# GpSimd instead of SyncE issues the transfers of the expert weights, with new orders of stages

## The chip, the cores and the metric

The kernel runs on one core of one Trainium2 chip. A core has five engines with an instruction stream each: TensorE (PE), VectorE (DVE), ScalarE (ACT), GpSimd (POOL) and SyncE (SP). SP computes nothing here; it issues DMAs. ACT and POOL can issue DMAs too. Each engine takes its stream in order: an instruction that waits for a semaphore holds up all that stand behind it on the same engine. The metric is device time in microseconds for one execution; lower is better.

## The reference

The program is two layers over eight sequences of 256 tokens with 128 features, all in float32. Cut to what matters:

```
xn = layernorm(x)
x  = x + attention_block(xn) + cell(xn)      # layer 0
xn = layernorm(x)
x  = x + mamba_block(xn) + moe(xn)           # layer 1

attention_block: 2 x (B=2, L=128 reshaped), 16 heads of 8, softmax(q k^T) + position table, Wo,
                 normalise, W1, W2, normalise
cell:            6 nodes in a chain; each: 8-head attention (q, k, v from earlier nodes),
                 output projection, weighted skip; layernorm at the end
mamba_block:     u = ln(x); in_proj; conv of 4 taps; silu; dt, B, C; scan over 16 states of
                 256 channels; gate; out_proj; + u; h = ln; gelu(h W1 + b1) W2 + b2; + residual
moe:             router over E = 8 experts, softmax(logits / 1.5), top 2 weights per token;
                 every expert is computed: h = silu(xn W1[e]); y = h W2[e];  out = sum_e w_e y
```

W1[e] and W2[e] are 128 x 512 and 512 x 128 floats, 256 KB each. Every expert is applied to every sequence, so 8 x 8 pairs of such matrices are brought in over the run.

## The kernel before

The eight sequences run as a pipeline. For each sequence b the work is cut into stages that stand in lanes (`CELL`, `SIDE`, `RAW`, `LAYER1`, `EXPERTS`, and `FOLD` once at the start). `ON` says which engines take part in a stage of a given name. For each engine the table `ORDER` holds one letter per stage: A to H are the cell's stages of sequences 0 to 7, a to h the key and value projections, I to P the attention block, i to p the mamba block and the FFN, Q to X the experts, and - the one-time folding. The function `order` takes the next stage of the letter's lane that this engine has a part in. So the order of work on each engine is fixed by hand or by a planner ahead of time, and the semaphores only make it correct. `BANKS` gives each use of a small PSUM bank its number (three banks `ps`), in TensorE's order.

The expert weights go through a ring of three buffers (`RING = 3`, tiles `w_e1` and `w_e2`, both called `w_e` in the trace). The stage `weights(b, e)` is number i = 8 b + e. It waits until the second product of expert i - 3 has been computed, since that frees the buffer, and then starts two transfers of 256 KB. TensorE's stage `expert(b, 2e)` waits for both of them:

```
def weights(b, e):
    i = b * EX + e
    if i == 0: sp.wait_ge(*fold_done.at(0, 2 * NODES - 1))
    if i >= RING: ready(sp, (i - RING) // EX, ("y", (i - RING) % EX))
    sp.dma_start(w_e1[:, i % RING, :], t["w_e1"][:, e, :]).then_inc(weights_in[i % RING], 16)
    sp.dma_start(w_e2[:, i % RING, :, :], ...).then_inc(weights_in[i % RING], 16)
```

In the trace these are SP's lines L623 and L624. Expert e's products are TensorE's lines L980 (first, stage `expert`) and L968 (second, stage `expert_y`, which frees the buffer).

What else SP issues: `load` and `store` of a sequence, the spreading of the attention block's heads through DRAM (`t_rows`, `a_write`, `a_stack`, `v_read`, `o_write`, `o_read`), and `rows` (L602), 128 times. `rows` closes a chain that every group of four heads goes through twelve or four times per sequence: TensorE computes scores into the four-bank PSUM tile `strips` (stage `max`, L772), VectorE takes their maximum (stage `top`, L1322, `rowmax`), TensorE transposes it (L779), ScalarE copies it out (L1080, `maxrow`), SP's `rows` moves its 4 KB into spare partitions of `qs_b` or `qs_a`, and TensorE computes the scores again with the maximum subtracted (stage `score`, L787). ScalarE then takes the exponential (stage `exp`, L1087, `probs`), which frees `strips`, and TensorE multiplies by the values (L800).

What GpSimd does: small operations that stand between two of VectorE. `root` (L1596) turns a variance into 1/sqrt for each of seven normalisations: `n0`, `n1` and `n2` are those of the second layer, and VectorE's `apply` (L1301) waits for it; `n1`'s result goes to TensorE's `z_t` (L882), `n2`'s to `h_t` (L936). `n0_apply` (L1625) and `x2` (L1661, L1663) sum residuals, `conv` (L1635) does the first tap, `dtx` (L1641) a product, and `state` (L1648, L1654, L1656) adds the halves of each pair of states; VectorE's `state(b, k)` (L1449) waits for the sum of pair k - 2.

## Time and profile before

| | |
|---|---|
| time, median of 3 executions | 1353.74 us (1352.81 to 1356.07) |
| the profiled execution | 1361.48 us |
| its span, first to last instruction | 1359.7 us |
| mean granted TensorE clock | 0.939 of full speed |
| PE busy | 1145.5 us, 84% |
| DVE busy | 988.0 us, 73% |
| ACT busy | 747.5 us, 55% |
| POOL busy | 272.9 us, 20% |
| expert weights | 128 transfers of 256 KB |

The profile is of one execution, so sums are made against its 1361.48 us; the median of the unprofiled ones is 7.7 us lower. Busy time counts neither waiting nor the issuing of DMAs. In a timeline row the number in brackets is the idle time of the engine ahead of the instruction, with what ended it.

### The profile page before, as it was taken

The page shows a single profiled execution, that of the slowest core. Times are in us where ns is not written, and L with a number is a line of the kernel's source. Part 1 is how long each engine was busy: PE and PEld are TensorE (multiplying, and loading weights), DVE is VectorE, ACT ScalarE, POOL GpSimd, SP SyncE. Part 2 cuts the span into 40 slices and gives each one's busy share as a digit, 9 for nine tenths or more (in the row PEclk, how much of TensorE's full clock was granted, in tenths as well). Part 3 has the DMA queues.
Part 4 walks back from the last instruction along what each step waited for, and adds up shares of the span by engine and source line. Part 5 has one row for each costly group of instructions (what it writes and reads, how often), then busy time and mean ns, then how long its engine had stood idle before and what let it go on. Part 6 is the DMA issues. An engine that isn't in the chain of part 4 may idle for free.

```text
span 1359.7 us, 27149 instructions
## 1 busy us (share of the span) xinstructions
PE 1145.5 (84%) x10384; PEld 781.7 (57%) x10384; DVE 988.0 (73%) x1563; ACT 747.5 (55%) x1325; POOL 272.9 (20%) x262
## 2 busy tenths in 40 slices
PE   6587768878988799988997899889998899888677
PEld 4354444545765567655764566656665567656455
DVE  3143245797678977897777877899677978788796
ACT  2233444664657565866567565665557565654442
POOL 1000002152022322043022232124112411023200
PEclk9787797889999899999999899899999899979799
DMA  7620011000310112110320031100310121002010
GB/s 210 145 60 1 2 39 23 2 17 29 95 40 17 28 68 57 35 33 17 75 68 2 17 81 42 52 32 28 92 37 2 48 76 52 33 32 71 4 62 20
DMA packets 117517, 62.66 MB, mean 46 GB/s; under 512 B 79440, under 2 KB 99440, under 8 KB 117392
## 3 DMA queue, kind: packets, MB, share of 16 engines
q1 hardware_dynamic: 113488, 54.68, 14.8%
q10 hardware_dynamic: 3904, 6.26, 1.4%
q8 instruction: 85, 1.39, 0.4%
q14 instruction: 40, 0.33, 0.1%
HBM read 53.56 MB, written 6.83 MB: 44 GB/s over the span
## 4 chain that ended last, share of the span: by engine, by line
PE 57%; DVE 20%; issue 10%; ACT 9%; DMA 3%; POOL 1%; SPq 0%; ACTq 0%; DVEq 0%; POOLq 0%
PE strips L787 9%; PE strips L772 8%; PE attn_out L800 7%; PE ps L968 6%; DVE rowmax_B L1322 6%; PE ps L980 6%; ACT probs L1087 4%; DVE hb L1457 3%; DVE rowmax_A L1322 2%; PE ps L823 2%; DVE hb L1449 2%; DVE hb L1464 2%; PE ps L911 2%; PE ps L730 2%; PE ps L890 1%
## 5 line engine op out<-in xcount | busy, mean ns | idle before, releaser
L1087 ACT ACTIVATE probs<-strips 128x2048 f32<-128x2048 f32 x128 | 240.2, 1877 | 108.8 <-PE strips L787 108.3
L1322 DVE TENSOR_REDUCE rowmax_B<-strips 128x8 f32<-128x2048 f32 x96 | 219.5, 2286 | 90.7 <-PE strips L772 89.8
L1457 DVE TENSOR_TENSOR_SCAN hb<-da,hb 128x1024 f32<-128x1024 f32 x64 | 156.9, 2452 | 2.5 <-ACT da L1171 0.8
L980 PE MATMUL ps<-ze,w_e 128*128 128x256 f32 x512 | 140.1, 403 | 8.8 <-DVE hb L1464 2.5
L787 PE MATMUL strips<-qs_b,ks_b 32*128 32x256 f32 x1536 | 120.4, 430 | 23.1 <-ACT probs L1087 13.0
L772 PE MATMUL strips<-ks_b,qs_b 32*128 32x256 f32 x1536 | 117.0, 420 | 26.0 <-ACT probs L1087 12.7
L968 PE MATMUL ps<-w_e,work 128*128 128x128 f32 x1024 | 133.0, 286 | 3.5 <-DVE hb L1449 1.1
L968 PEld LDWEIGHTS ps<-w_e,work 128*128 128x128 f32 x1024 | 126.6, 200 | 13.7 <-issue 10.5
L1171 ACT ACTIVATE da<-dt,a_neg 128x255 f32<-128x255 f32 x256 | 108.0, 498 | 24.3 <-DVE hb L1457 23.9
L1654 POOL TENSOR_TENSOR cv_t<-hb 128x512 f32<-128x512 f32 x49 | 62.4, 1273 | 275.5 <-DVE hb L1464 275.5
L1218 ACT ACTIVATE eh_t<-ps 128x512 f32<-128x512 f32 x128 | 74.8, 594 | 74.7 <-PE ps L980 74.0
L980 PEld LDWEIGHTS ps<-ze,w_e 128*128 128x128 f32 x512 | 93.2, 197 | 38.5 <-issue 19.9
L1561 DVE SCALAR_TENSOR_TENSOR work<-eh_t,ps 128x512 f32<-128x512 f32 x128 | 85.3, 678 | 36.0 <-ACT eh_t L1218 35.7
L800 PE MATMUL attn_out<-probs,vb 128*32 128x256 f32 x1536 | 108.3, 404 | 0.6 <-ACT probs L1087 0.2
L772 PEld LDWEIGHTS strips<-ks_b,qs_b 32*128 32x128 f32 x1536 | 75.0, 194 | 52.9 <-issue 48.1
L787 PEld LDWEIGHTS strips<-qs_b,ks_b 32*128 32x128 f32 x1536 | 76.6, 199 | 48.1 <-issue 30.9
L1656 POOL TENSOR_TENSOR cv<-cv,cv_t 128x512 f32<-128x512 f32 x49 | 92.0, 1878 | 3.8
L1080 ACT ACTIVATE maxrow<-ps 8x128 f32<-8x128 f32 x128 | 33.7, 264 | 105.8 <-PE ps L779 104.0
L1322 DVE TENSOR_REDUCE rowmax_A<-strips 128x8 f32<-128x2048 f32 x32 | 73.1, 2286 | 24.6 <-PE strips L772 24.5
L1464 DVE TENSOR_TENSOR hb<-hb,ps 128x1024 f32<-128x1024 f32 x64 | 77.7, 1214 | 13.6 <-PE ps L911 12.9
L1449 DVE TENSOR_TENSOR hb<-ps,dtx 128x1024 f32<-128x1024 f32 x64 | 78.0, 1218 | 12.3 <-PE ps L911 11.2
L800 PEld LDWEIGHTS attn_out<-probs,vb 128*32 128x32 f32 x1536 | 41.7, 113 | 47.6 <-issue 24.1
(239 smaller groups left out, 1825.7 us busy)
## 6 DMA issues: line engine op xcount, KB each, us to landing
w_e<-in_w_e SPq DMA_DIRECT2D x128, 256.0 KB, 2.9
qs_a<-a_scr SPq DMA_DIRECT2D x8, 512.0 KB, 3.8
ks_a<-a_scr SPq DMA_DIRECT2D x8, 512.0 KB, 4.9
pos<-t_scr ACTq DMA_DIRECT2D x16, 192.0 KB
a_scr<-qkv_a SPq DMA_DIRECT2D x16, 128.0 KB, 4.3
qs_b<-maxrow SPq DMA_DIRECT2D x96, 4.0 KB
x_in<-in_x SPq DMA_DIRECT2D x8, 128.0 KB, 2.4
a_scr<-ks_a SPq DMA_DIRECT2D x2, 512.0 KB, 6.5
```

The costliest lines, as they stand in the source:

```text
L772: mm = pe.matmul(o, strip(qs, b, kind, g, j, qc * P, P), strip(ks, b, kind, g, j, 0, L), start=True, stop=True)
L787: mm = pe.matmul(o, strip(ks, b, kind, g, j, kc * P, P), strip(qs, b, kind, g, j, 0, L), start=True, stop=True)
L800: mm = pe.matmul(attn_out[32 * j:32 * j + 32, i * L:(i + 1) * L], v, heads[:, j, kc, :], start=(kc == 0), stop=(kc == 1))
L968: mm = pe.matmul(o[:, h * D:(h + 1) * D], eh[:, e % 2, j, h * P:(h + 1) * P], w_e2[:, (b * EX + e) % RING, j, :], start=(j == 0), stop=(j ...
L980: mm = pe.matmul(o[:, j * L:(j + 1) * L], w_e1[:, n % RING, f * P:(f + 1) * P], ze[:, b % 2, :], start=True, stop=True)
L1087: act.activation(probs[:, group % 2, :, :, :].rearrange("p h a b -> p (h a b)"), strips[:, :], ACT.Exp).then_inc(s_exp, 1)
L1171: last = act.activation(da[:, k % 2, m, j, 1:L], dt[:, m, 1:L], ACT.Exp, scale=a_neg[:, m, 2 * k + j:2 * k + j + 1])
L1322: dve.tensor_reduce(out=rowmax[kind][:, b % sides_n, k % 2, :, :], in_=strips[:, :].rearrange("p (h q t) -> p h q t", h=4, q=2), axis=AX, ...
L1449: dve.tensor_tensor(hk, o, dtx[:, :, :].unsqueeze(2).to_broadcast([P, CH, 2, L]), ALU.mult).then_inc(hb_done.of(b), 1)
L1457: dve.tensor_tensor_scan(flat_h, flat_a, flat_h, 0.0, ALU.mult, ALU.add).then_inc(scan_done.of(b), 1)
L1464: dve.tensor_tensor(hk, hk, o, ALU.mult).then_inc(hc_done.of(b), 1)
L1656: pool.tensor_tensor(ysum[:, :, :], ysum[:, :, :], pair[:, :, :], ALU.add).then_inc(ysum_done.of(b), 1)
```

## The change

`weights` moves from SP to GpSimd. The function is the same but for the engine: it waits for the same semaphores and starts the same two transfers with the same counts. No computation is added or removed. With it come new tables `ORDER` for all five engines and new `BANKS`.

```diff
 ON = {
-    "sync": "load rows t_rows a_write a_stack v_read o_write o_read weights store",
+    "sync": "load rows t_rows a_write a_stack v_read o_write o_read store",
...
-    "gpsimd": "consts prep_root xn_bo end_root ... conv dtx state x2",
+    "gpsimd": "consts prep_root xn_bo end_root ... conv dtx state x2 weights",
...
 ORDER = {
     "sync": (
-        "IAAAIIIIIIJJJJJABBQAQQIIBAAI...
+        "IAAIAIIIIIJJJJJAABBIAIAIBAAAAI...
...
     "gpsimd": (
-        "ABIJCK-IIIIAAiiiDLiiiiiiiiiiiiJJBJBJjjjEM...
+        "ABIJCQQQ-IIKIIAAiiiDLiiiiiiiQiiQiiiQQQJJRBJBJRjjjEM...
...
-                sp.dma_start(w_e1[:, i % RING, :], t["w_e1"][:, e, :]).then_inc(weights_in[i % RING], 16)
-                sp.dma_start(w_e2[:, i % RING, :, :], t["w_e2"][:, FF * e:FF * e + FF, :]).then_inc(weights_in[i % RING], 16)
...
+                    pool.wait_ge(*fold_done.at(0, 2 * NODES - 1))
+                if i >= RING:
+                    ready(pool, (i - RING) // EX, ("y", (i - RING) % EX))
+                pool.dma_start(w_e1[:, i % RING, :], t["w_e1"][:, e, :]).then_inc(weights_in[i % RING], 16)
+                pool.dma_start(w_e2[:, i % RING, :, :], t["w_e2"][:, FF * e:FF * e + FF, :]).then_inc(weights_in[i % RING], 16)
```

Leaving the 64 `weights` stages out, the number of stages that stand at another place in their engine's sequence is 97 of 216 on SP, 455 of 1362 on TensorE (126 of them by two places or more, the farthest by 16), 303 of 921 on ScalarE, 170 of 842 on VectorE (by at most 6) and 19 of 185 on GpSimd. Three places of these sequences follow. Lines behind the removed function have other numbers in the changed kernel: GpSimd's L1596 is L1587 there, L1625 is L1616, L1635 is L1626, L1661 and L1663 are L1652 and L1654; its L1662 and L1663 are the two transfers.

SP, near the start: in the kernel before, the first three `weights` stages stand among the `rows` of sequences 0 and 1.

```order
35 L575 DMA a_scr<-qkv_a 128x16x16 x2
36 L576 DMA v_scr<-qkv_a 128x256
37 L602 DMA qs_b<-maxrow 4x2x128 x2
38 L623 DMA w_e<-in_w_e 128x512
39 L624 DMA w_e<-in_w_e 128x512
40 L602 DMA qs_b<-maxrow 4x2x128
41 L623 DMA w_e<-in_w_e 128x512
42 L624 DMA w_e<-in_w_e 128x512
43 L623 DMA w_e<-in_w_e 128x512
44 L624 DMA w_e<-in_w_e 128x512
45 L602 DMA qs_a<-maxrow 4x2x128 x2
```

In the changed kernel, at the same place:

```order
37 L575 DMA a_scr<-qkv_a 128x16x16 x2
38 L576 DMA v_scr<-qkv_a 128x256
39 L602 DMA qs_b<-maxrow 4x2x128 x3
40 L602 DMA qs_a<-maxrow 4x2x128
41 L602 DMA qs_b<-maxrow 4x2x128
42 L602 DMA qs_a<-maxrow 4x2x128
```

Nothing stands between these index transfers any more.

GpSimd, the first two normalisations of layer 1 of sequence 6 (`n0_root`, `n0_apply`, `n1_root`, then `conv`). Before:

```order
217 L1596 TENSOR_TENSOR rstd_n<-veps_n,half_neg 128x2
218 L1625 TENSOR_TENSOR res<-x,u 128x256
219 L1596 TENSOR_TENSOR rstd_n<-veps_n,half_neg 128x2
220 L1635 TENSOR_SCALAR cv<-xi,convw 128x256 x2
221 L1641 TENSOR_TENSOR dtx<-dt,xc 128x512
```

Changed:

```order
313 L1587 TENSOR_TENSOR rstd_n<-veps_n,half_neg 128x2
314 L1616 TENSOR_TENSOR res<-x,u 128x256
315 L1662 DMA w_e<-in_w_e 128x512
316 L1663 DMA w_e<-in_w_e 128x512
317 L1662 DMA w_e<-in_w_e 128x512
318 L1663 DMA w_e<-in_w_e 128x512
319 L1587 TENSOR_TENSOR rstd_n<-veps_n,half_neg 128x2
320 L1662 DMA w_e<-in_w_e 128x512
321 L1663 DMA w_e<-in_w_e 128x512
322 L1626 TENSOR_SCALAR cv<-xi,convw 128x256 x2
```

The stages `weights(6, 0)` and `weights(6, 1)` now stand between the sum of the residual and the root of `n1`, and `weights(6, 2)` behind it.

GpSimd, the end of layer 1's mamba block of sequence 4 (`x2`, then `n2_root`). Before:

```order
177 L1661 TENSOR_TENSOR res<-res,u 128x256
178 L1663 TENSOR_TENSOR res<-res,rows 128x256
179 L1596 TENSOR_TENSOR rstd_n<-veps_n,half_neg 128x2
180 L1596 TENSOR_TENSOR rstd_wo<-veps_wo,half_neg 128x2
181 L1610 TENSOR_TENSOR ab_bias<-rem_a,bias_ff 128x256
```

Changed:

```order
251 L1652 TENSOR_TENSOR res<-res,u 128x256
252 L1654 TENSOR_TENSOR res<-res,rows 128x256
253 L1662 DMA w_e<-in_w_e 128x512
254 L1663 DMA w_e<-in_w_e 128x512
255 L1587 TENSOR_TENSOR rstd_n<-veps_n,half_neg 128x2
256 L1662 DMA w_e<-in_w_e 128x512
257 L1663 DMA w_e<-in_w_e 128x512
```

`weights(4, 5)` now stands ahead of the root of `n2`, and `weights(4, 6)` behind it.

## Rows read from the trace of the kernel before

**Rows 1.** The page: busy time of engines, and shares of the ending chain.

```profile
PE 1145.5 (84%) x10384; PEld 781.7 (57%) x10384; DVE 988.0 (73%) x1563; ACT 747.5 (55%) x1325; POOL 272.9 (20%) x262
PE 57%; DVE 20%; issue 10%; ACT 9%; DMA 3%; POOL 1%; SPq 0%; ACTq 0%; DVEq 0%; POOLq 0%
```

**Rows 2.** The page, DMA issues: count, KB each, us to landing (median).

```profile
w_e<-in_w_e SPq DMA_DIRECT2D x128, 256.0 KB, 2.9
```

**Rows 3.** Timeline of SP from 85.9 us: start, duration, engine, line, operation.

```profile
85.90 0.36 SPq L623 DMA_DIRECT2D w_e<-in_w_e  x1
86.30 0.43 SPq L624 DMA_DIRECT2D w_e<-in_w_e  x1
86.77 0.53 SPq L602 DMA_DIRECT2D qs_b<-maxrow  x1
```

**Rows 4.** Timeline of ACT at the same place, then of PE.

```profile
83.09 0.27 ACT L1080 ACTIVATE maxrow<-ps 8x128 f32<-8x128 f32 x1 [1.10 <-PE ps L779]
85.32 1.88 ACT L1087 ACTIVATE probs<-strips 128x2048 f32<-128x2048 f32 x1 [0.72 <-PE strips L787]
...
89.18 2.09 PE L787 MATMUL strips<-qs_b,ks_b 32*128 32x256 f32 x16 [1.78 <-DMA qs_b<-maxrow]
```

**Rows 5.** Timelines near 632 us (ACT, SP, PE) and near 785 us (ACT, PE).

```profile
631.75 0.27 ACT L1080 ACTIVATE maxrow<-ps 8x128 f32<-8x128 f32 x1 [1.91 <-PE ps L779]
...
632.49 0.53 SPq L602 DMA_DIRECT2D qs_b<-maxrow  x1
...
635.27 0.93 PE L787 MATMUL strips<-qs_b,ks_b 32*128 32x256 f32 x12 [1.21 <-DMA qs_b<-maxrow]
...
783.83 1.88 ACT L1087 ACTIVATE probs<-strips 128x2048 f32<-128x2048 f32 x1 [0.85 <-PE strips L787]
...
785.85 0.93 PE L787 MATMUL strips<-qs_b,ks_b 32*128 32x256 f32 x12 [1.87 <-ACT probs L1087]
```

**Rows 6.** The waits: who for whom, us in total, times, longest.

```profile
PEld strips L787 <- DMA qs_b<-maxrow: 11.4, 11, 2.0
```

**Rows 7.** POOL by line (busy us, mean ns), then one tile (ns min/median/max).

```profile
L1596 POOL TENSOR_TENSOR rstd_n<-veps_n,half_neg 128x2 f32<-128x2 f32 x24 | 16.9, 704 | 21.9 <-DVE veps_n L1296 21.1
...
L1656 POOL TENSOR_TENSOR cv<-cv,cv_t x49: 1259/1271/3148, 280.0 to 1254.7; 128x512 f32<-128x512 f32 x49
```

**Rows 8.** Timelines of POOL, PE and DVE, 1134 to 1143 us (sequence 6).

```profile
1134.88 0.73 POOL L1625 TENSOR_TENSOR res<-x,u 128x256 f32<-128x256 f32 x1 [0.82 <-DVE u L1301]
1136.46 0.70 POOL L1596 TENSOR_TENSOR rstd_n<-veps_n,half_neg 128x2 f32<-128x2 f32 x1 [0.86 <-DVE veps_n L1296]
...
1135.47 1.95 PE L968 MATMUL ps<-w_e,work 128*128 128x128 f32 x16
...
1142.38 0.38 PE L882 MATMUL ps<-ident,z_tm 128*128 128x128 f32 x2
...
1138.51 0.59 DVE L1301 TENSOR_SCALAR z_tm<-u,mv_n,rstd_n 128x128 f32<-128x128 f32 x2
```

**Rows 9.** Timelines of POOL and PE, 948 to 951 us (sequence 4).

```profile
948.25 0.72 POOL L1663 TENSOR_TENSOR res<-res,rows 128x256 f32<-128x256 f32 x1
949.08 0.70 POOL L1596 TENSOR_TENSOR rstd_n<-veps_n,half_neg 128x2 f32<-128x2 f32 x1
...
950.75 0.44 PE L936 MATMUL ps<-ident,z_tm 128*128 128x128 f32 x2
```

**Rows 10.** Timelines of POOL and PE, 846 to 852 us (expert 7, sequence 3).

```profile
846.64 0.69 POOL L1596 TENSOR_TENSOR rstd_prep<-veps_prep,half_neg 128x2 f32<-128x2 f32 x1 [1.78 <-DVE veps_prep L1296]
...
850.89 1.46 PE L980 MATMUL ps<-ze,w_e 128*128 128x256 f32 x6
```

**Rows 11.** Timelines of PE and DVE, 459 to 472 us (sequence 1).

```profile
459.93 3.75 PE L968 MATMUL ps<-w_e,work 128*128 128x128 f32 x16 [0.45 <-ACT maxrow L1080]
...
471.49 1.23 DVE L1449 TENSOR_TENSOR hb<-ps,dtx 128x1024 f32<-128x1024 f32 x1
```

85 lines of the change are left out of this document (41 added, 44 removed).

## The prediction, made before the changed kernel was run

> **What bounds the kernel.** I read the page first: PE is busy 84% of the span, DVE 73%, POOL 20%, and of the chain that ended last PE holds 57%, DVE 20%, DMA 3%, POOL 1% and SP's own issuing nothing that shows [rows 1]. So no single engine is saturated, but TensorE is close, and whatever makes it idle, or makes VectorE idle ahead of a stage that feeds it, is time. Both engines run in a fixed order, so a stage that comes late holds up all behind it, whether or not other work is ready. POOL's 20% says only that it has room; it doesn't say that it has room at the right moments, and that is the question here. Next I read the transfers: 128 of 256 KB, landing 2.9 us after their issue [rows 2]. In the waits nobody waits for one of them, so bringing the weights in is hidden today. The change can therefore help only through what stood behind the weights on SP, and can hurt only through what stands behind them on POOL, through weights that arrive later, and through the new orders.
>
> **SP is freed.** The change takes 64 stages off SP, with two issues of 0.36 and 0.43 us each [rows 3], and the wait ahead of them. Of the 128 index transfers `rows`, 34 stand directly behind such a pair. The clearest case is at the start. ScalarE had the row ready at 83.09 + 0.27 = 83.36 us, but SP stood in `weights(0, 0)` until 85.9 and issued it at 86.77. TensorE began the scores at 89.18 after 1.78 us of idleness, which this transfer ended [rows 3, 4]. Now the index goes out at 83.4 and is there 2.41 us later (89.18 - 86.77), at 85.8. What is late next is `strips`: the exponential holds it until 85.32 + 1.88 = 87.20 [rows 4], and TensorE's earlier work ended at 89.18 - 1.78 = 87.40. So the whole gap goes: -1.8 us. A second case is near 632 us: row ready at 632.02, issued at 632.49, a gap of 1.21 us in TensorE [rows 5]. The lag is the smaller, so this gives -0.5. The third that looks like one is not: near 785 us the gap of 1.87 us was ended by the exponential, which ran until 785.71 [rows 5]; an earlier index changes nothing there. The other `rows` behind a pair were issued in time or have their `score` well behind. Sum on SP: -2.3 us.
>
> **The price of an issue on POOL.** No DMA is issued from POOL in this trace. From below: SP's issue, 0.43 us [rows 3]. It cannot be less, or the weights would be issued for nothing. From above: the longest operation that POOL shows, 3.13 to 3.15 us, where the same addition otherwise takes 1.27 [rows 7]. I take 1.1 us: the smallest arithmetic on POOL, on 2 elements per partition, takes 0.70 [rows 7], which is what an instruction costs there before it does anything, and 0.4 for the issue itself. A stage of two issues is then 2.2 us, and 64 of them are 141 us, so POOL goes from 20% to some 30%. Most of that lies in time when POOL waits anyway. The last word of a pair lands 2.9 - 0.43 = 2.5 us behind the second issue [rows 2, 3].
>
> The Trainium skill, "DMA: Bandwidth & Descriptors", section Specifications, gives a first byte after about 1 us for the GpSimd path and about 0.6 us for SyncE's. By that estimate each landing would be 0.4 us later than I count, which would add 0.4 us to the sum below; no row here shows it.
>
> **Where it lies on POOL's path.** For each of the 64 stages I set the moment at which its buffer comes free against the operation that now stands behind it on POOL. In most places nobody notices. An example: `weights(1, 4)` stands ahead of `state(1, 4)` and has to wait for a product that ended at 459.93 + 3.75 = 463.68. POOL's pair sum comes out at 463.68 + 2.2 + 1.27 = 467.2. The one who waits for it is VectorE's `state(1, 6)`, at 471.49 [rows 7, 11]. 4 us are left, so it costs nothing; with 3.13 us an issue it would be 471.2, still just nothing. Three places are different.
>
> First, sequence 6, 1135 us [rows 8]. `weights(6, 0)` begins when the residual sum is done, 1134.88 + 0.73 = 1135.61, and ends at 1137.81. `weights(6, 1)` may begin at 1135.47 + 1.95 = 1137.42, so it follows at once and ends at 1140.01. `n1_root` ends at 1140.71. VectorE used it at 1138.51, so VectorE stands still for 2.2 us, with the experts' gating and the next maximum queued behind, for which TensorE waits in turn. TensorE's `z_t` at 1142.38 has itself moved a few places forward, so it hides nothing. +2.2 us.
>
> Second, sequence 4, 949 us [rows 9]. `weights(4, 5)` begins at 948.25 + 0.72 = 948.97, its buffer being long free, and `n2_root` starts at 951.17 instead of 949.08. VectorE's scaling follows in the same instant, and TensorE's `h_t` came at 950.75, directly on its heels. +2.1 us. That expert 5 itself (just behind `h_t`) gets its weights at 951.17 + 2.5 = 953.7 lies mostly under the same delay.
>
> Third, sequence 3, 847 us [rows 10]. `weights(3, 7)` is issued only behind the root of another sequence, at 846.64 + 0.69 = 847.33, and lands at 847.33 + 2.2 + 2.5 = 852.03. TensorE wants it at 850.89. +1.1 us.
>
> Sum on POOL: +5.4 us. With 0.43 us an issue the three are 0.5, 0.9 and 0: +1.4. With 3.13 us they are 10.3, 6.2 and 5.2: +21.7.
>
> **The new orders.** 455 of TensorE's 1362 stages and 170 of VectorE's 842 have moved, nearly all by a place or two among neighbours that don't depend on each other. At the start the order of TensorE is practically the old one, and the attention block of sequence 0 has the same transfers ahead of it. I find no place where a large gap is closed or opened. I count zero, with bounds on both sides: a neighbour in the wrong place costs, or gives back, a gap such as 1.78, 1.21 or 1.87 us [rows 4, 5], and some five more of one sign than of the other are easily possible, so 8 us each way.
>
> **Sum.** -2.3 + 5.4 + 0 = +3.1 us. The profiled execution took 1361.5 us, which becomes 1364.6; the median of the runs is 7.7 us lower, 1353.7, which becomes 1357 us. With the lowest price it is 1353.7 - 2.3 + 1.4 = 1352.8.
>
> **Rivals.**
>
> POOL's issues are dear (slower). If each takes as long as a blocked POOL operation, 3.13 us, the sum is 1353.7 - 2.3 + 21.7 = 1373 us, and places that I count as hidden come to light too. For it: the 3.15 us in rows 7 are the same operation as the 1.26 us ones, so POOL can be held up by something outside of it. Against it: the median there is 1.27, so most are not. It decides from about 1.3 us an issue on, where the result passes 1358. The Trainium skill, "SBUF — State Buffer", section SBUF: two separate sides, states a rule of this sort against the change: a DMA from the GpSimd queue has its descriptors written by GpSimd, which can't write them while VectorE holds the port that they share, whereas those from SyncE are immune. By that rule alone the result would be this rival's 1373; no run so far shows a DMA under it.
>
> The index transfers gain much more (faster). TensorE's loading of weights for L787 waited 11.4 us in 11 places for them [rows 6]. If a queue free of 256 KB transfers in front lets all of that go, and if half of the 8 us of the orders comes on top, it is 1353.7 - 11.4 - 4 + 3 = 1341 us. Against it: I found only two of these waits behind a pair; the others are the transfer's own time.
>
> SP was never in the way (no change). The transfers run on the same DMA engines whoever starts them, and if both POOL's delays and SP's lags are taken up by the slack between stages, the time stays at 1354. The Trainium skill, "DMA: Bandwidth & Descriptors", section Issuing engines are not separate DMA queues, says just this: another issuing engine saves only the time to initiate.
>
> The orders decide (either sign): 1353.7 ± 8, 1346 or 1362.
>
> **Chances.** A measurement of this kernel can tell about 0.3%, 4.1 us, from no change. My forecast (1352.8 to 1360) gets 0.40: 0.24 within 0.3%, 0.14 slower, 0.02 faster. Dear issues 0.20, all slower. Index transfers 0.16, all faster. No change 0.09. The orders 0.15: 0.06 faster, 0.02 within, 0.07 slower. Together: faster 0.24, same 0.35, slower 0.41. The range has to take in the upper price and most of the faster cases: 1343 to 1374.
>
> **What would show it.** Right: SP shows no wait of L623's kind and `score(0, 3)` starts near 87.4 us instead of 89.2; POOL's transfers take about 1.1 us each, POOL's busy time with them is near 410 us; `n1_root` of sequence 6 and `n2_root` of sequence 4 stand directly behind an issue and VectorE has a gap of some 2 us ending on them; TensorE waits a few us in all for `w_e`, where it waited for none. Wrong: issues of 2 us or more, or of very unequal length beside VectorE's scans (the dear rival); waits of L787 for the index gone altogether (the faster one); or gaps of TensorE that moved to lines which have to do with neither SP nor POOL, in which case the orders decided and my zero for them was the mistake.

## The result

The changed kernel took 1361.00 us (median of 5 runs, 1360.25 to 1363.86) against 1353.74 (1352.81 to 1356.14, 5 runs) before. The ratio is 1.0047, with a 95% interval of 1.0029 to 1.0066: slower by about 6.4 us by the ratio (the two medians lie 7.3 us apart), which is more than 0.3%, and 4 us above the predicted 1357.

The two profiled executions, 1360.8 us after and 1361.5 before, don't show this. The one before lies 7.7 us above its median, at a mean granted clock of 0.939, the one after at 0.953. A single execution of this kernel scatters: 35 runs of the kernel before on one chip spread from 1349.2 to 1364.1 us (standard deviation 3.5 us). So what follows compares medians for the sum, and traces only for stretches that repeat from one execution to the next.

The page of the changed kernel: busy time by engine, then the chain that ended last [answers to rows 1], then the transfers of the weights by issue and by queue [rows 2].

```profile
PE 1131.6 (83%) x10384; PEld 768.2 (57%) x10384; DVE 985.9 (73%) x1563; ACT 747.5 (55%) x1325; POOL 346.3 (25%) x390
...
PE 51%; DVE 20%; issue 11%; ACT 10%; DMA 5%; POOL 2%; SPq 0%; ACTq 0%; DVEq 0%; POOLq 0%
...
w_e<-in_w_e POOLq DMA_DIRECT2D x128, 256.0 KB, 3.1
```

PE's busy time fell by 13.9 us (1145.5 to 1131.6), as less of it ran at the half clock, and the time did not: the span less the busy time, PE's idleness, rose from 214.2 to 227.4 us. POOL has 128 instructions and 73.4 us more, 0.57 us for each. The queue's share of the chain is small throughout.

The transfers by line, with durations in ns (minimum, median, maximum); L1662 is the first and L1663 the second issue of a stage. Below L1663: who waited for it, and how long its landing took:

```profile
L1662 POOL DMA_DIRECT2D w_e<-in_w_e x64: 536/579/701, 85.8 to 1335.3; - x64
...
L1663 POOL DMA_DIRECT2D w_e<-in_w_e x64: 536/536/555, 86.5 to 1335.9; - x64
...
  PEld ps L971: 0.6, 1
  PE ps L971: 0.4, 1
...
DMA to landing us min/median/max: 3.0/3.3/6.2
```

An issue takes 0.54 to 0.58 us, half of the 1.1 that I had counted, and never more than 0.70. This speaks against the dear rival. The Trainium skill, "SBUF — State Buffer", section SBUF: two separate sides, has GpSimd kept from writing descriptors while VectorE runs an operation in a two-port mode. None of the 128 issues here shows it, and no landing took more than 6.2 us, where SyncE's took up to 5.1 us in the kernel before and up to 7.6 with the new orders. Whether an issue ever met such an operation was not looked up, so this doesn't test the rule.

The first place of SP (timelines of ACT, SP, PE and POOL, start and duration in us), to be held against rows 3 and 4:

```profile
82.66 0.27 ACT L1071 ACTIVATE maxrow<-ps 8x128 f32<-8x128 f32 x1 [1.10 <-PE ps L770]
82.95 1.14 SPq L602 DMA_DIRECT2D qs_b<-maxrow  x2
...
86.91 1.15 PE L778 MATMUL strips<-qs_b,ks_b 32*128 32x256 f32 x16
...
85.76 0.70 POOL L1662 DMA_DIRECT2D w_e<-in_w_e  x1 [41.06 <-DVE bias_v L1242]
86.46 0.54 POOL L1663 DMA_DIRECT2D w_e<-in_w_e  x1
```

SP now issues the index 0.02 us behind the row instead of 3.4, and `score(0, 3)` starts at 86.91 instead of 89.18. In the waits, TensorE's loading of weights waited 4.7 us in 8 places for such an index, against 11.4 in 11 [rows 6]. Most of this fall isn't SyncE's freedom. The new orders with the weights on SyncE (below) have 4.2 us in 6 places, and start `score(0, 3)` without a wait too, since SyncE's own new order has the weights behind the index; the move alone has 7.1 in 10. And the same wait for the other tile, `qs_a`, grew:

```profile
PEld strips L787 <- DMA qs_a<-maxrow: 3.8, 4, 1.5
```

```profile
PEld strips L778 <- DMA qs_a<-maxrow: 6.5, 5, 1.7
```

So of 15.2 us for both tiles 11.2 are left.

### The profile page after: what moved, and what is told of

The parts are those of the page before. It is cut to its first block, busy times and chain, and to the rows that moved or that the text cites. A ratio compares the mean times of both kernels' runs of the same rounds, so it can differ in the third digit from the quotient of the medians.

```text
span 1359.0 us, 27149 instructions
## 1 busy us (share of the span) xinstructions
PE 1131.6 (83%) x10384; PEld 768.2 (57%) x10384; DVE 985.9 (73%) x1563; ACT 747.5 (55%) x1325; POOL 346.3 (25%) x390
## 3 DMA queue, kind: packets, MB, share of 16 engines
q0 software_dynamic: 10240, 33.56, 7.2%
## 4 chain that ended last, share of the span: by engine, by line
PE 51%; DVE 20%; issue 11%; ACT 10%; DMA 5%; POOL 2%; SPq 0%; ACTq 0%; DVEq 0%; POOLq 0%
PE strips L778 8%; PE strips L763 8%; PE attn_out L791 6%; DVE rowmax_B L1313 5%; PE ps L959 5%; ACT probs L1078 4%; PE ps L971 4%; DVE rowmax_A L1313 2%; PE ps L814 2%; DVE hb L1448 2%; DVE hb L1440 1%; PE ps L902 1%; ACT da L1162 1%; PE attn_out L798 1%; DVE hb L1455 1%
## 5 line engine op out<-in xcount | busy, mean ns | idle before, releaser
L1448 DVE TENSOR_TENSOR_SCAN hb<-da,hb 128x1024 f32<-128x1024 f32 x64 | 152.8, 2388 | 2.4 <-ACT da L1162 0.8
L959 PE MATMUL ps<-w_e,work 128*128 128x128 f32 x1024 | 128.3, 279 | 2.9 <-ACT ze L1128 0.8
L959 PEld LDWEIGHTS ps<-w_e,work 128*128 128x128 f32 x1024 | 122.1, 193 | 12.8 <-issue 10.5
L1647 POOL TENSOR_TENSOR cv<-cv,cv_t 128x512 f32<-128x512 f32 x49 | 94.3, 1925 | 3.8
L1440 DVE TENSOR_TENSOR hb<-ps,dtx 128x1024 f32<-128x1024 f32 x64 | 78.1, 1220 | 16.5 <-PE ps L902 13.9
L1662 POOL DMA_DIRECT2D w_e<-in_w_e x64 | 36.7, 573 | 157.4 <-PE ps L959 47.1
```

Of the source, the lines that this page charges most:

```text
L959: mm = pe.matmul(o[:, h * D:(h + 1) * D], eh[:, e % 2, j, h * P:(h + 1) * P], w_e2[:, (b * EX + e) % RING, j, :], start=(j == 0), stop=(j ...
L1440: dve.tensor_tensor(hk, o, dtx[:, :, :].unsqueeze(2).to_broadcast([P, CH, 2, L]), ALU.mult).then_inc(hb_done.of(b), 1)
L1448: dve.tensor_tensor_scan(flat_h, flat_a, flat_h, 0.0, ALU.mult, ALU.add).then_inc(scan_done.of(b), 1)
L1647: pool.tensor_tensor(ysum[:, :, :], ysum[:, :, :], pair[:, :, :], ALU.add).then_inc(ysum_done.of(b), 1)
```

## Undoing it part by part

The orders can be cut. At many points the same stages lie ahead of the point in both orders, on all five engines at once, so that a kernel can run the one order up to there and the other behind it. I used a point at 846 us of the changed kernel's trace (VectorE about to start `inproj` of sequence 4). The tables below are one row of `ORDER` each; the other engines' rows and `BANKS` go with them.

**The kernel before once more**, for the scatter of traces.

> The kernel before, unchanged, profiled a second time. The first profiled execution took 1361.5 us, 7.7 us over the median of its kernel, with a mean granted clock of 0.939; the changed kernel's took 1360.8 with 0.953. If the first was merely an execution with a low clock, this one comes out near 1354 us with a clock of 0.945 or more, and the 7 us between the two kernels are to be read against it. If profiled executions of this kernel are always longer, it comes out near 1361 again, and the comparison of the two traces on record (equal spans) is a fair one.

It took 1356.72 us, span 1354.9, 4.8 us shorter than the first trace of the same kernel, at a mean granted clock of 0.938: neither of the two outcomes expected. The difference comes in steps of either sign, of 0.6 to 3.1 us from the end of one `ffn_out` to the next.

**The move alone**: GpSimd issues, old orders and old banks.

```diff
 ORDER = {
 ...
-        "TPUmmUmmmUmUUmmmmmUmUNNNUNFFnnnVVnVnnnnVVnnnVnnnnVVOOGOOGooWWoWooWooWWoooWPWPooXXPoXPHHoopppppXXXXXpppppppppp",
+        "TPUmmUmmmUmUUmmmmmUmUNNNUNFFnnnVVnVnnnnVVnnnVnnnnVVOOGOGOooWWoWooWooWWoooWPWPooXXPoXPHHoopppppXXXXXpppppppppp",
 ...
```

> The move alone: the weights are issued by GpSimd, with the orders of before on TensorE, ScalarE, VectorE and SyncE (less the 64 weights stages) and its PSUM banks; on GpSimd the stages stand in the order of before, with the weights behind the same neighbours as in the changed kernel. Theory A (the new orders cost the time, the move is free: an issue took 0.54 to 0.58 us and nobody waited for weights but 1 us): 1351 to 1356 us, a ratio of 0.998 to 1.002 to before. Rival B (the move costs it, through what waits on GpSimd behind a weights stage): 1359 to 1363 us. If each has a part, between them.

**The new orders alone**: SyncE issues, new orders and banks.

```diff
 ORDER = {
 ...
-        "nnnOOGOGOooooooooooPPooPoPHHooppppppppppppppp",
+        "nnnOOGOOGooooooooooPPooPoPHHooppppppppppppppp",
 ...
```

> The orders alone: the new orders of the changed kernel on TensorE, ScalarE, VectorE and GpSimd and its PSUM banks, but the weights issued by SyncE, standing among its other stages by the moments at which GpSimd issued them in the trace of the changed kernel. Theory A (the new orders cost the time): 1359 to 1363 us. Rival B (the move costs it): 1352 to 1356 us.

The move alone gave 1359.59 us, ratio 1.0027 (1.0005 to 1.0048). The new orders alone gave 1362.65, ratio 1.0054 (1.0033 to 1.0076). Both together are the changed kernel, 1.0047. So the orders alone already make the whole loss, theory A of that run, and with them in place the move adds nothing that can be seen. But the move in the old orders is not free, as theory A of its run had it: its interval lies above 1, and its time is that of rival B. The two parts don't simply add (0.27 and 0.54% against 0.47 together), though the difference, 0.34%, is about as large as its uncertainty. In the orders-alone kernel the weights stand at new places on SyncE, too, so it holds the whole of the new order and not the old places of the weights. Stage by stage against the trace of the kernel before, both kernels with new orders were ahead at 850 us and behind at 1125, hence the next pair.

**New orders up to 846 us, old behind it** (GpSimd issues; a row of SyncE's order against the changed kernel):

```diff
-        "MNMNEEOOOOONFHFNTGFFGNFFNGFFNONOGOUGGOPPPPPHHGGGGOOGGHOOPPHPHVHPPHHPHHPPHHWX",
+        "MNMNEEOOOOONFHFTNGFFGFNFNGFOFNNGOPPPPPOGUGHHOGGGGOOPGGHOOHPPVHHPPHHPHHPPHHWX",
```

> The new orders and banks up to 846 us (the place where VectorE goes on to sequence 4's inproj), the old ones from there; weights issued by GpSimd throughout. The traces of the changed kernel and of the new orders with SyncE both lie ahead of the kernel before at 850 us (12.6 and 6.3 us) and behind it at 1125 us (1.5 and 6.2). Theory A (the new orders gain early and lose in 850 to 1125): the early gain stays and the late loss goes, about 1351, between 1347 and 1355. Rival B (the differences of the traces are the spread of single executions and the clock, not the orders): as the changed kernel, 1359 to 1362. Rival C (the loss is what the early gain turns into, because something later waits on a rate that no order moves): 1357 to 1361 as well, but with the milestone at 850 us ahead and the one at 1125 us not.

**Old up to 846 us, new behind it**:

```diff
-        "MNMNEEOOOOONFHFNTGFFGNFFNGFFNONOGOUGGOPPPPPHHGGGGOOGGHOOPPHPHVHPPHHPHHPPHHWX",
+        "MMNENOOOOOENFFHNTGFFGNFFNGFFNONOGOUGGOPPPPPHHGGGGOOGGHOOPPHPHVHPPHHPHHPPHHWX",
```

> The mirror image: old orders and banks up to 846 us, new ones from there; weights issued by GpSimd throughout. Theory A: no early gain, and the whole late loss of 8 to 12 us: 1364 to 1369. Rival B: 1359 to 1362. Rival C (a rate that no order moves): 1357 to 1361.

They gave 1356.70 us, ratio 0.9989 (0.9969 to 1.0010), and 1365.36, ratio 1.0056 (1.0034 to 1.0078). The late half of theory A holds: the same issuing engine, the same set of stages, and 0.67% between the two halves put together in the one way and in the other. B and C, which gave the second kernel at most 1362, fall. The early half of A isn't shown: the first kernel missed its 1347 to 1355, its ratio includes 1, and in its trace sequence 3 ends at 835.6 us, where the kernel before has 836.1 and 835.4.

**New up to 846 us, old behind it, SyncE issues**:

```diff
-        "MEMNNNNNMTTGTFEFSEMEETMFFETEMMMNENTOOOOOENTFFHTUTNUGUFFGUUFNFNUUGFOFUNNGOPPPPPVOGUGVHVHOGGGVGOVVOPGGHOOVVHPPWWWVHHPWWPHHWPWHHPPWHXHXXWXXXXXX",
+        "MMNNNNSNMFTGTTFEESMEEMFFTETEMMNMNEEOOOOOTTNFHFTUTNUGUFFGUUFNFNUUGFOFUNNGOPPPPPVOGUGVHVHOGGGVGOVVOPGGHOOVVHPPWWWVHHPWWPHHWPWHHPPWHXHXXWXXXXXX",
```

> As the run with the new orders up to 846 us and the old ones from there, but with the weights issued by SyncE, at the places of the new-orders-with-SyncE kernel in the early part and of the kernel before in the late one. Theory A with a move that costs 0.2 to 0.3% in the late old order: 1350 to 1353, below the kernel before (1355 to 1357 in its runs here). Rival (the early orders gain only together with the move, since SyncE is then free): as before, 1354 to 1358.

1355.24 us, ratio 0.9994 (0.9970 to 1.0018). The expected 1350 to 1353 did not come, the rival's 1354 to 1358 did. It is no faster than the kernel before, and no version in this study is.

With seven kernels, the one before included, each part of the change can be priced three times, as the difference of two ratios that differ in it alone:

| part | pairs | mean |
|---|---|---|
| new orders behind 846 us | +0.29, +0.58, +0.60% | +0.49%, +6.6 us |
| new orders up to 846 us | -0.38, -0.09, -0.06% | -0.18%, -2.4 us |
| GpSimd issues | +0.27, -0.05, -0.07% | +0.05%, +0.7 us |

One difference is uncertain by some 0.3%, a mean of three by not quite 0.2%. So the late part is shown, and the early part and the move are each not told from nothing (the one price of the move that stands clear of nothing by itself is that in the old orders, +0.27%). The traces say the same of the late part. Us by stretch, from one end of `ffn_out` to the next (each row a single execution):

| kernel | to 3 | 3 to 4 | 4 to 5 | 5 to 7 |
|---|---|---|---|---|
| before, its two traces | 836.1, 835.4 | 129.6, 128.6 | 159.9, 160.5 | 230.8, 227.1 |
| move alone | 832.3 | 131.2 | 162.4 | 233.8 |
| new then old, GpSimd | 835.6 | 130.5 | 160.9 | 227.4 |
| new then old, SyncE | 830.7 | 129.4 | 161.2 | 228.4 |
| old then new, GpSimd | 830.2 | 132.6 | 166.0 | 226.2 |
| new orders, SyncE | 833.8 | 131.5 | 166.5 | 226.8 |
| changed kernel | 827.5 | 131.1 | 168.5 | 228.7 |

From `ffn_out` of sequence 4 to that of 5, the last three rows, which run it in the new orders, are 3.6 to 8.6 us above all others. That is the stretch to read. From 3 to 4 they are longer too against those with the same issuing engine, by 1.0 us on average with GpSimd and 2.3 with SyncE, and from 5 to 7 there is nothing to see within the scatter.

## What happens in the stretch: sequence 5, `bc`

Set against the end of `ffn_out(4)`, the traces of one order agree stage by stage to 0.1 us for long stretches there. Us by part of the stretch on TensorE (each row a single execution; idle is TensorE's):

| kernel | `ffn_out(4)` to `bcdt(5)` | of it idle | to `state(5, 0)` | to `ffn_out(5)` |
|---|---|---|---|---|
| before, its two traces | 53.4, 53.4 | 3.9, 3.9 | 12.0, 12.0 | 94.5, 95.1 |
| move alone | 53.4 | 3.9 | 14.8 | 94.3 |
| new then old, GpSimd | 53.4 | 3.9 | 12.0 | 95.5 |
| new then old, SyncE | 53.4 | 3.9 | 14.8 | 93.1 |
| old then new, GpSimd | 55.0 | 5.2 | 16.3 | 94.8 |
| new orders, SyncE | 55.2 | 5.7 | 16.0 | 95.3 |
| changed kernel | 56.3 | 5.2 | 16.8 | 95.4 |

The two orders part most in the middle, where the old order itself has 12.0 or 14.8 us depending on the clock, and by 1.6 to 2.9 us before it, in several small waits. The middle holds the one place that the next four runs test. TensorE, timelines of the move alone (old order) and of the changed kernel. L770 is the transpose of a row of maxima, L890 the first product of `bcdt(5)`:

```profile
1016.72 0.27 PE L770 MATMUL ps<-ident,rowmax_A 128*8 128x128 f32 x1
1016.83 0.27 PE L770 MATMUL ps<-ident,rowmax_B 128*8 128x128 f32 x1
1016.93 1.03 PE L890 MATMUL ps<-xc,w_bc 128*96 128x256 f32 x4
```

```profile
1014.77 0.27 PE L770 MATMUL ps<-ident,rowmax_A 128*8 128x128 f32 x1
1014.88 1.03 PE L890 MATMUL ps<-xc,w_bc 128*96 128x256 f32 x4
```

The new order has put `rows(7, B, 1)` behind `max(6, B, 7)`, so `bcdt(5)` starts 0.1 us earlier relative to VectorE's maximum ahead of it. A harmless step forward. But `bcdt` releases two things: VectorE's `bc`, which stands behind that maximum and starts no earlier, and ScalarE's `dt`, which releases POOL's `dtx`, and that is 0.1 us earlier. VectorE and POOL in the kernel before, then in the changed one:

```profile
1022.77 0.42 DVE L1430 TENSOR_TENSOR bc<-cv,cv_t 32x256 bf16<-32x256 f32 x1
...
1022.83 1.48 POOL L1641 TENSOR_TENSOR dtx<-dt,xc 128x512 f32<-128x512 f32 x1 [17.04 <-ACT dt L1160]
...
1025.65 1.15 PE L787 MATMUL strips<-qs_a,ks_a 32*128 32x256 f32 x16 [2.59 <-DVE rowmax_B L1322]
```

```profile
1018.64 1.50 DVE L1421 TENSOR_TENSOR bc<-cv,cv_t 32x256 bf16<-32x256 f32 x1
...
1018.59 1.26 POOL L1632 TENSOR_TENSOR dtx<-dt,xc 128x512 f32<-128x512 f32 x1 [16.45 <-ACT dt L1151]
...
1022.60 1.15 PE L778 MATMUL strips<-qs_a,ks_a 32*128 32x256 f32 x16 [3.58 <-DVE rowmax_B L1313]
```

Before, VectorE's last operation of `bc` began 0.06 us ahead of POOL's product and took 0.42 us (POOL's took 1.48). After, POOL began 0.05 us ahead, and the same operation on 32x256 elements took 1.50 us. The maximum of sequence 6 stands behind it, TensorE waits for that, and its idleness rises from 2.59 to 3.58 us. The Trainium skill, "SBUF — State Buffer", section Who interferes with whom, says that a VectorE instruction with two inputs in SBUF contends with a GpSimd one that reads SBUF, and that issue order decides which of the two blocks; the trace agrees, with 0.42 and 1.50 us for the two orders. (GpSimd's product took 1.26 us where it began first and 1.48 where VectorE did.) In the four traces with the new order at this place (the changed kernel, new with SyncE, old then new, and the one with four issues, below) the longest of these operations is 1.50 us; in all those with the old order there it is 0.42.

Behind this, the clock. Windows from that start of TensorE to the end of `state(5, 0)`: the stretch and its length, busy us (instructions) of PE, PEld, DVE, ACT and POOL, granted clock, DMA share, GB/s. In order: before, the move alone, the changed kernel.

```profile
1025.65:1031.20 5.55, 5.33 (x58) 3.42 (x58) 0.22 (x1) 4.46 (x9) 0.00 (x0) 1.00 0.01 3
```

```profile
1023.47:1031.73 8.26, 8.26 (x60) 5.16 (x61) 1.28 (x2) 4.93 (x10) 0.00 (x0) 0.62 0.01 2
```

```profile
1022.60:1031.67 9.07, 8.46 (x59) 4.42 (x59) 1.28 (x2) 5.20 (x10) 0.00 (x0) 0.62 0.01 3
```

The same work takes 5.55 us at 1.00 (2.4 GHz) and 8.26 at 0.62 (part of it at 1.2 GHz). Since the move alone fell too, after the very idleness of 2.60 us that left the kernel before at 1.00, the longer idleness isn't what takes the clock down, or not alone. The next runs separate the two.

**`dtx` of sequence 5 waits for the end of `bc`** (changed kernel):

```diff
             def dt_x(b):
                 pool.wait_ge(*dt_done.at(b))
+                if b == 5:
+                    pool.wait_ge(*bc_steps.at(b, 4))
```

> The changed kernel with one wait added: in sequence 5 GpSimd's dtx product starts only after VectorE's last operation of bc (L1421). In the four traces that end in the new orders (the changed kernel, new orders with SyncE, old then new, four issues) this 32x256 operation of sequence 5 took 1.50 us where the traces with the old late order show 0.42, GpSimd's dtx having begun 0.05 us ahead of it; PE then sat idle 3.6 us ahead of score A 1 of sequence 6 instead of 2.6, and the granted clock was 0.5 for some 5 us behind it. Theory D (that operation is held up by GpSimd's beside it, and the longer idle takes the clock down; both together are some 4 us of the late loss): L1421 at 0.42 us in every sequence, the idle at 2.6 us, the clock at 1.00, the stretch from the end of ffn_out of sequence 4 to state 0 of sequence 5 shorter by 4, and the whole 1357, about 4 below the changed kernel's 1361. Rival E (the 1.1 us come back but the clock falls all the same, other work in the new order being what makes PE idle): stretch shorter by 1 to 2, whole 1359 to 1360. Rival F (whatever is gained there is taken back behind it): stretch shorter, whole 1361.

Its line, TensorE's start behind it, and the window from that start:

```profile
L1421 DVE TENSOR_TENSOR bc<-cv,cv_t x8: 416/416/418, 247.6 to 1288.3; 32x256 bf16<-32x256 f32 x8
...
1024.59 1.45 PE L778 MATMUL strips<-qs_a,ks_a 32*128 32x256 f32 x16 [2.50 <-DVE rowmax_B L1313]
...
1024.59:1033.44 8.85, 8.59 (x59) 4.51 (x59) 1.29 (x2) 5.20 (x11) 0.00 (x0) 0.61 0.01 3
```

The hold-up is gone (0.42 us), the idleness is back at 2.50, and from `bcdt(5)` to `state(5, 0)` it takes 15.49 us instead of 16.79. The clock fell all the same, to 0.61. So at this place E is right and D isn't: 1.1 us of idleness come back, and the clock is a matter of its own. Further on the trace tells no more: from `ffn_out(4)` to `ffn_out(5)` it takes 168.8 us, the changed kernel 168.5, since 1.7 us more went by ahead of `bcdt(5)`, where the added wait can't act and more of the time was at the half clock. In the whole, 1363.19 us and a ratio of 1.0038 (1.0018 to 1.0058) don't tell 1.1 us from nothing, nor E from F.

**The delay put into the kernel before**:

```diff
                 dve.wait_ge(*bc_steps.at(b, 3))
+                if b == 5:
+                    dve.wait_ge(*dtx_done.at(b))
```

> The kernel before (old orders, SyncE) with the delay put in by hand: in sequence 5 VectorE's last operation of bc waits for GpSimd's dtx, so that it ends some 1.6 us later (dtx ran to 1.1 us behind the end of bc, and 0.4 for the operation itself). Theory D: PE's idle ahead of score A 1 of sequence 6 grows from 2.6 to about 4.2 us, the clock falls to 0.5 behind it, the stretch from ffn_out of sequence 4 to state 0 of sequence 5 is 4 to 5 us longer, and the whole 1358 to 1360 against 1355. Rival E (the delay costs its own length and the clock stays): stretch 1.6 longer, whole 1356.6. Rival F (taken back behind it): 1355.

```profile
1026.99 1.61 PE L787 MATMUL strips<-qs_a,ks_a 32*128 32x256 f32 x9 [4.02 <-DVE rowmax_B L1322]
...
1026.99:1033.75 6.76, 6.76 (x58) 4.20 (x58) 0.49 (x1) 4.61 (x9) 0.00 (x0) 0.77 0.01 2
```

The idleness is 4.02 us, the clock 0.77 in the window, and from `bcdt(5)` to `state(5, 0)` it takes 14.72 us instead of 12.01: the delay of 1.4 and 1.3 of lost clock. That the delay took the clock down isn't shown, since it fell as well in five of the eight traces of the old order without the delay. At the end of the kernel nothing of it is left in the trace (0.5 us less than the first trace of before); 1359.55 us, ratio 1.0013 (0.9989 to 1.0037), takes in D, E and F and settles none.

**`dtx` waits in all sequences, new then old, SyncE**. In the old late order another such meeting stands in sequence 4, where `dtx` begins inside `bc`, which then takes 2.90 us instead of 1.95. The new order doesn't have that one: its `bc` takes 1.95 us in sequence 4 and 3.03 in sequence 5, the old one's 2.90 and 1.95. So over both sequences the meetings of `bc` and `dtx` cost the two orders nearly the same, 1.1 us against 0.95, and they explain the stretch from 4 to 5 better than the loss of the whole.

```diff
                 pool.wait_ge(*dt_done.at(b))
+                pool.wait_ge(*bc_steps.at(b, 4))
```

> The run before with GpSimd's dtx waiting for the end of VectorE's bc in all sequences. In the old late order bc of sequence 4 takes 2.90 us instead of 1.95 since dtx begins inside it; with the wait it should take 1.95, and dtx start 1.9 us later in sequence 4 and 0.35 later in sequences 5 and 6. Theory D: 1 us gained at sequence 4 and nothing lost, so 0 to 1.5 us below its twin; rival (dtx late holds up state 0): 0 to 2 us above it.

1355.67 us, ratio 0.9993 (0.9972 to 1.0014), against 0.9994 without the wait. Its trace takes 128.4 us from `ffn_out` 3 to 4, its twin's 129.4, with `bc` of sequence 4 at 1.95 us, as theory D has it. The medians don't tell the theories apart.

**The old orders put back from 966 to 1125 us alone** (changed kernel, a row of SyncE's order):

```diff
-        "MNMNEEOOOOONFHFNTGFFGNFFNGFFNONOGOUGGOPPPPPHHGGGGOOGGHOOPPHPHVHPPHHPHHPPHHWX",
+        "MNMNEEOOOOONFHFNTGFFGNFFNGFFNONGOPPPPPOGUGHHOGGGGOOPGGHOOHPPHVHPPHHPHHPPHHWX",
```

> The changed kernel with the old orders and banks put back in one stretch alone, from 966 us (ffn_out of sequence 4) to 1125 us (ffn_out of sequence 5); before and behind it the new ones, weights on GpSimd. In the traces this stretch is 6.1 to 9.1 us longer than in the kernel before in the four kernels that run it in the new orders and -0.1 to 2.6 longer in those that run it in the old ones without a delay put in. Theory A (the late loss lies in this stretch): 1354 to 1357, 4 to 7 below the changed kernel's 1361. Rival (the loss lies elsewhere behind 846 us, or what is gained here is taken back by 1258 us): 1359.5 to 1362, with the stretch itself shorter.

The stretch shrank as expected, from 168.5 to 163.0 us. The whole did so by half: 1359.76 us, ratio 1.0020 (0.9999 to 1.0042). Theory A's 1354 to 1357 did not come; the time is that of the rival, which had the stretch shorter and the whole at 1359.5 to 1362. Against the changed kernel's 1.0047 it is 0.27% less, with an uncertainty of some 0.3%, so that between none and all of the late 0.49% can be in this stretch. The rest, if there is one, is behind 846 us in places that I have not found; the table points at 3 to 4, where this trace, too, takes 133.4 us.

Within the stretch I read the loss of some 6 us in the traces as a sum of pieces, of which only the first was tested by a run: 1.1 us of `bc`; 0.6 us where TensorE's second expert product waits for ScalarE (the new order has put `rows(7, B, 1)` behind an exponential there); two further steps of 0.5 to 0.7 and one of 1.5 near `wo_y` of sequences 5 and 6; and the half clock, which came in all five traces that run `bc(5)` in the new order (the one with the wait included) and in six of the nine with the old one, too few to call it the order's.

The largest of TensorE's waits that differ is `wo_y`'s, for the attention block's heads coming back from DRAM. Over the stretch: the move alone, the new orders with SyncE, the changed kernel (the kernel before has none).

```profile
PE ps L850 <- DMA va_hd<-o_scr: 1.1, 1, 1.1
PE ps L859 <- DMA va_hd<-o_scr: 2.9, 2, 2.1
PE ps L850 <- DMA va_hd<-o_scr: 2.0, 2, 1.6
```

In the old orders this is a cost of the move that neither the prediction nor the expectations had. Sequence 6 in the kernel before, then in the move alone:

```profile
1105.33 0.34 SPq L608 DMA_DIRECT2D o_scr<-out_hd  x1
1107.14 0.36 SPq L614 DMA_DIRECT2D va_hd<-o_scr  x1
1107.56 1.14 SPq L623 DMA_DIRECT2D w_e<-in_w_e  x1
```

```profile
1103.20 0.59 POOL L1662 DMA_DIRECT2D w_e<-in_w_e  x1
1104.54 0.34 SPq L608 DMA_DIRECT2D o_scr<-out_hd  x1
1107.77 0.37 SPq L614 DMA_DIRECT2D va_hd<-o_scr  x1
1112.05 0.71 PE L850 MATMUL ps<-waq,va_hd 128*128 128x128 f32 x4 [1.09 <-DMA va_hd<-o_scr]
```

On SyncE the weights stand behind `o_write` (L608) and `o_read` (L614). On GpSimd a pair goes out 1.3 us ahead of `o_write`, which then lands 3.1 us after its issue instead of 1.7; `o_read` waits for that landing and takes 4.2 us itself instead of 3.0. All four kernels with the old order there and GpSimd issuing have this wait (0.9 to 1.1 us), none of the five with SyncE does. No run took it away by itself.

## GpSimd's path: two more runs

**Roots first.** Where an issue stood right ahead of a short POOL stage, that stage goes first (14 stages of weights, 12 places), with the old orders; against the move alone:

```diff
-        "TPUmmUmmmUmUUmmmmmUmUNNNUNFFnnnVVnVnnnnVVnnnVnnnnVVOOGOGOooWWoWooWooWWoooWPWPooXXPoXPHHoopppppXXXXXpppppppppp",
+        "PTUmmUmmmUmUUmmmmmmUUNNNNUFFnnnVVnVnnnnVVnnnVnnnnVVOOGOGOoooWWWooWooWWoooWPPWooXXPoPXHHoopppppXXXXXpppppppppp",
```

> The orders of before with GpSimd issuing the weights, and wherever an issue stood right ahead of a root or another short GpSimd stage that DVE waits for (14 stages of weights in 12 places, n1_root of sequence 6 and n2_root of sequence 4 among them) that stage goes first. Against the move alone with the old orders, 1359.6. Theory P (the move's cost lies in GpSimd stages that run 1.1 to 2.2 us late behind the issues): 1355 to 1357, as before. Rival Q (these places cost nothing, the 4 us are elsewhere or are spread): 1358.5 to 1361.

It took 1362.69 us, ratio 1.0031 (1.0005 to 1.0057), no better than the move alone; P falls. Why shows at sequence 4, which I had named. POOL and PE in the move alone, then PE with the root first:

```profile
945.49 0.55 POOL L1663 DMA_DIRECT2D w_e<-in_w_e  x1
946.06 0.72 POOL L1587 TENSOR_TENSOR rstd_n<-veps_n,half_neg 128x2 f32<-128x2 f32 x1
...
948.79 1.13 PE L971 MATMUL ps<-ze,w_e 128*128 128x256 f32 x4 [0.88 <-DMA w_e<-in_w_e]
```

```profile
953.02 2.07 PE L971 MATMUL ps<-ze,w_e 128*128 128x256 f32 x4 [2.57 <-DMA w_e<-in_w_e]
```

Both the root and the weights are wanted there at once. With the issue first the root is 1.1 us late, TensorE is idle for 0.65 us ahead of `h_t`, and even so waits 0.88 us for the weights; with the root first it waits 2.57 us for them. From `ffn_out` 3 to 4 the old order took 128.4 to 129.7 us in the five traces with SyncE, 130.5 and 131.2 with GpSimd, and 134.5 with the roots first. So the place costs some 1.7 us, 1.5 of it in these two waits, and can't be mended by turning it round: the weights wait on POOL behind a residual that came at 943.45, which SP never did.

**Four issues instead of two** (changed kernel, 128 KB each, halves of the partitions):

```diff
-                    pe.wait_ge(weights_in[n % RING], 32 * (n // RING + 1))
+                    pe.wait_ge(weights_in[n % RING], 64 * (n // RING + 1))
 ...
-                pool.dma_start(w_e1[:, i % RING, :], t["w_e1"][:, e, :]).then_inc(weights_in[i % RING], 16)
-                pool.dma_start(w_e2[:, i % RING, :, :], t["w_e2"][:, FF * e:FF * e + FF, :]).then_inc(weights_in[i % RING], 16)
+                for h in (slice(0, 64), slice(64, 128)):
+                    pool.dma_start(w_e1[h, i % RING, :], t["w_e1"][h, e, :]).then_inc(weights_in[i % RING], 16)
+                    pool.dma_start(w_e2[h, i % RING, :, :], t["w_e2"][h, FF * e:FF * e + FF, :]).then_inc(weights_in[i % RING], 16)
```

> The changed kernel with each of the two transfers of a stage cut into two by partitions (64 each), so that GpSimd issues four of 128 KB where it issued two of 256 KB: same bytes, 128 more issues, at 0.56 us each 72 us more of GpSimd. Against the changed kernel, 1361.0. Theory P: each place where a root stands behind the issues is late by twice as much, sequence 6 by 2.2 us more and sequence 4 by 1.1 more: 1363 to 1366. Rival Q (the issues lie beside idle time or slack): 1359.5 to 1362.

It took 1377.22 us, ratio 1.0150 (1.0115 to 1.0185): 14 us above the changed kernel, where theory P gave 2 to 5. Waits (us in all, times, longest) that grew, the changed kernel first:

```profile
PEld strips L778 <- DMA qs_b<-maxrow: 4.7, 8, 1.1
DVE z_tm L1292 <- POOL rstd_n L1587: 5.8, 9, 0.9
```

```profile
PE 1133.0 (83%) x10384; PEld 770.0 (56%) x10384; DVE 987.3 (72%) x1563; ACT 748.3 (54%) x1325; POOL 406.0 (30%) x518
...
PEld strips L778 <- DMA qs_b<-maxrow: 9.6, 10, 1.7
DVE z_tm L1292 <- POOL rstd_n L1587: 9.1, 12, 2.0
PEld ps L971 <- DMA w_e<-in_w_e: 2.0, 2, 1.2
```

POOL is busy 60 us longer, and the delay grows all along the kernel in steps of about 1 us. My three places are among them. In sequences 4 and 6 VectorE and TensorE now wait as theory P has it:

```profile
955.35 0.44 PE L927 MATMUL ps<-ident,z_tm 128*128 128x128 f32 x2 [1.59 <-DVE z_tm L1292]
1156.42 0.60 DVE L1292 TENSOR_SCALAR z_tm<-u,mv_n,rstd_n 128x128 f32<-128x128 f32 x2 [1.95 <-POOL rstd_n L1587]
1157.76 0.41 PE L873 MATMUL ps<-ident,z_tm 128*128 128x128 f32 x2 [1.89 <-DVE work L1552]
```

(The last one ends with VectorE's `work`, which stands right behind the late scaling.) In the changed kernel TensorE's two gaps are 0.62 and under 0.1 us, so the root costs 1.0 and 1.8 us more (P: 1.1 and 2.2); at the third place, expert 7 of sequence 3, its wait for the weights grew from 0.41 to 0.99 us. P's mechanism is there, then, but it is some 3 of the 14 us. An issue on POOL is not free; the first 128 nearly were, the second 128 cost 14 us. How much of this is POOL's time and how much the other shape of the transfers (64 partitions, 12288 packets in place of 10240) was not separated.

## Why the prediction was right in part

The time lay in the range and the direction had the largest chance, but the sum +3.1 was put together wrongly, and that it came within 4 us is luck: the loss is the orders', which it had at zero. By its own steps:

- **SP is freed, -2.3 us: right where it was named.** `score(0, 3)` moved from 89.18 to 86.91 us (forecast 87.4), and to 86.97 in the move alone; part of that is not SP's, since the second trace of before has it at 88.40. Near 632 us the lag fell from 0.48 to 0.03 us, and TensorE's gap in the move alone from 1.21 to 0.81. But the first gap goes as well in the new orders with SyncE (86.24), by the order alone. Whether this reaches the end can't be read from the medians.
- **An issue on POOL, 1.1 us: too dear by half.** It is 0.54 to 0.58. I had taken POOL's smallest arithmetic, 0.70 us, as a floor and put the issue on top; an issue isn't an arithmetic operation and is shorter than one. POOL stands at 346 us busy, not 410.
- **Three places, +5.4 us: 2.3 us in the old orders, 1.0 in the changed kernel.** Sequence 6: the root is late as described, and in the move alone VectorE waits 1.15 us for it (below), but TensorE's `z_t` comes only 0.6 us later against its surroundings, not 2.2. In the changed kernel no wait shows there. Sequence 4: 1.7 us instead of 2.1, in the old orders; there half of it is the landing of the weights, which I had set aside as hidden under the root's delay. In the changed kernel it is 0.62 us. Sequence 3: in the changed kernel TensorE waits 0.41 us for the weights of expert 7 instead of 1.1, in the move alone under 0.1. With 0.55 us an issue the same working gives 0.7, 1.0 and 0.0 us for the three, so the price of an issue is the term that was mis-sized. (With 0.43 us the second place is 948.97 + 0.86 - 949.08 = 0.75 us and not 0.9, which makes the lowest sum 1352.6 instead of 1352.8.) What the working left out is the wait of `wo_y` behind the weights, 0.9 to 1.1 us in the old orders: I had asked what stands behind the weights on POOL, and not what their transfers run beside.

```profile
1139.31 0.72 POOL L1587 TENSOR_TENSOR rstd_n<-veps_n,half_neg 128x2 f32<-128x2 f32 x1
1140.14 0.60 DVE L1292 TENSOR_SCALAR z_tm<-u,mv_n,rstd_n 128x128 f32<-128x128 f32 x2 [1.15 <-POOL rstd_n L1587]
1143.35 0.38 PE L873 MATMUL ps<-ident,z_tm 128*128 128x128 f32 x2
```

- **The move as a whole, +3.1 us: +0.7 by the three pairs**, with an uncertainty of some 2.5 us that just includes both; in the old orders alone, for which the working was made, it is +0.27%, 3.7 us. That this is near 3.1 is partly luck, since an issue was counted twice too dear and the wait of `wo_y` not at all.
- **The new orders, 0 us: this is the step that failed.** They are +6.6 us behind 846 us and -2.4 ahead of it, about +4 together. I had looked for large gaps that a swap opens or closes and found none. What the traces show in their place is many small ones: TensorE's idleness ahead of `bcdt(5)` grew from 3.9 to between 5.2 and 5.7 us without a single wait above 1 us, a shift of 0.1 us turned round which of two engines begins first and cost 1.1, and `wo_y` waits 2.0 to 2.9 us for its transfer. My own sign for being wrong, gaps of TensorE that moved to lines which have to do with neither SP nor POOL, applies in part only: `dtx` is POOL's, and the transfer that `wo_y` waits for is SP's. The rival "the orders decide" (1362, 0.07 on the slow side) is what happened, and its chance was too small for a change that moved a third of TensorE's stages.
- **Rivals that fell:** the dear one (issues of 3.13 us) by their maximum of 0.70; the gain by index transfers, since the waits for both tiles together fell by 4.0 of 15.2 us only, those for `qs_b` fell as far with the weights on SyncE, and the time did not follow.

What stays open: where the late loss lies outside the stretch from 4 to 5, and which of its small pieces come with the order and which with the execution; why the clock falls at `bc(5)` in some executions of the old order; and whether the early gain is real. In the early part something did change: averaged over its executions, the granted clock of each kernel with the new early orders is 0.947 to 0.950, leaving the one with four issues aside (0.943), and 0.939 to 0.942 for each with the old ones. PE is busy for 1130 to 1140 us in the traces of the former, and for 1145 to 1153 in those of the latter but one (old then new, 1136). Its idleness grew by most of that, and of the gain 2.4 us are left, which are not told from nothing.

## What to carry to other kernels

When a change comes with a regenerated order, run the order without the change and the change without the order before explaining anything: here the order alone was +0.54%, the change on top of it -0.07%, and the change without the order +0.27%. Orders that share cut points can be bisected like code, and single traces, useless for the sum here, agree to 0.1 us inside a stretch. Moving DMA issues to a less busy engine moves them behind that engine's waits too; ask for each what stands ahead of it there, not only what stands behind, and which small transfers on the old queue it may now run ahead of.
